# Weighing node rows by counted edges: the counts become the stationary operand behind the first piece

## The reference, cut to what matters

```python
def _L0_gnn_ref(mems, r, W, y, edge_index):
    ...
    deg = jax.ops.segment_sum(w, col, num_segments=MEM_LEN) + SELF_LOOP_W
    dinv = jax.lax.rsqrt(deg)
    norm = dinv[row] * w * dinv[col]
    xw = mems2 @ W
    msg = norm[:, None] * xw[row]
    out = jax.ops.segment_sum(msg, col, num_segments=MEM_LEN)
    out = out + (SELF_LOOP_W * dinv * dinv)[:, None] * xw
    return out
...
x = x + _L0_gnn_ref(_layernorm(x, axis=-1), ...)
x = x + _L0_ffn_ref(_layernorm(x, axis=-1)[None], ...)[0]
```

## Time and profile before

| | us |
|---|---|
| median of three runs | 2783.07 |
| lowest, highest | 2780.23, 2785.92 |
| the profiled execution: its span, first to last instruction | 3123.0 |
| PE, PEld, DVE, ACT, POOL busy in it | 2109.3, 1813.6, 1410.3, 561.5, 1730.5 |

### The profile page before, as it was taken

One profiled execution on the slowest core, in us unless ns is written; L12 is line 12 of the kernel. 1 busy time (PEld: TensorE's weight loads), 2 busy tenths in 40 slices (PEclk: granted clock), 3 DMA queues, 4 the chain that ended last, 5 costly groups with the idle time before them and its releaser, 6 DMA issues. The chain is left out here.

```text
span 3123.0 us, 39685 instructions
## 1 busy us (share of the span) xinstructions
PE 2109.3 (68%) x12106; PEld 1813.6 (58%) x12107; DVE 1410.3 (45%) x3867; ACT 561.5 (18%) x1062; POOL 1730.5 (55%) x1774
## 2 busy tenths in 40 slices
PE   2002665775677657756768868887488689799964
PEld 1002444774466546745757767777477578688754
DVE  5897766225531552254152134444543344344422
ACT  0046100110011001101101112222112223233211
POOL 5731366666666666666666656666034534544354
PEclk7555888988889889888988888998799899899987
DMA  9114222553245325524544556665302212211221
GB/s 238 47 55 142 66 87 88 162 173 93 88 135 177 118 88 162 179 87 128 176 124 151 178 154 188 193 185 177 112 26 61 67 31 66 64 38 64 62 37 23
DMA packets 231940, 350.57 MB, mean 112 GB/s; under 512 B 38888, under 2 KB 165128, under 8 KB 231620
## 3 DMA queue, kind: packets, MB, share of 16 engines
q0 software_dynamic: 79808, 198.30, 22.0%
q1 hardware_dynamic: 151796, 149.91, 15.5%
q10 hardware_dynamic: 144, 0.20, 0.0%
HBM read 296.73 MB, written 56.40 MB: 113 GB/s over the span
## 5 line engine op out<-in xcount | busy, mean ns | idle before, releaser
L633 POOL DMA_INDIRECT arena<-z_table,arena x1248 | 1221.5, 979 | 768.6 <-issue 337.3
L1598 PE MATMUL bank<-arena 128*128 128x128 f32 x4992 | 782.5, 316 | 90.2 <-issue 74.0
L1598 PEld LDWEIGHTS bank<-arena 128*128 128x128 f32 x4992 | 736.7, 228 | 149.8 <-issue 126.8
L1166 DVE TENSOR_TENSOR nodes<-nodes,bank 128x256 f32 x312 | 131.7, 422 | 1076.5 <-remote 749.6
L1609 PE MATMUL bank<-arena 128*128 128x490 bf16 x496 | 169.7, 429 | 313.1 <-DVE arena L1177 287.0
L1823 PE MATMUL bank<-arena 128*128 128x256 f32 (+1 forms) x1472 | 334.1, 385 | 27.1 <-ACT arena L837 24.9
L1811 PE MATMUL bank<-arena 128*128 128x256 f32 (+1 forms) x1472 | 334.9, 388 | 25.2 <-issue 18.6
L1621 PE MATMUL bank<-arena 128*128 128x128 f32 (+1 forms) x1960 | 289.9, 290 | 74.9 <-issue 65.4
L694 POOL DMA_INDIRECT out<-arena x128 | 129.8, 1014 | 355.5 <-DVE arena L1483 343.5
L1811 PEld LDWEIGHTS bank<-arena 128*128 128x128 f32 x1472 | 285.8, 198 | 68.2 <-issue 28.2
L1823 PEld LDWEIGHTS bank<-arena 128*128 128x128 f32 (+1 forms) x1472 | 276.3, 190 | 71.6 <-ACT arena L837 26.9
(11 more groups left out here) (299 smaller groups left out, 1767.5 us busy)
## 6 DMA issues: line engine op xcount, KB each, us to landing
arena<-z_table SPq DMA_DIRECT2D x120, 512.0 KB
arena<-z_table,arena POOLq DMA_INDIRECT x1248
arena<-in_L_ffn_w SPq DMA_DIRECT2D x16, 1024.0 KB
z_table<-nodes SPq DMA_DIRECT2D x14, 896.0 KB, 6.7
x_rows<-nodes SPq DMA_DIRECT2D x98, 128.0 KB
arena<-in_x SPq DMA_DIRECT2D x48, 256.0 KB
out<-nodes SPq DMA_DIRECT2D x96, 128.0 KB
nodes<-in_x SPq DMA_DIRECT2D x12, 896.0 KB, 8.3
```

The costliest lines, as they stand in the source:

```text
L633: nc.gpsimd.indirect_dma_start(gath[:, slot, t, :], None, z_table, bass.IndirectOffsetOnAxis(ap=src_idx[:, tile_at:tile_at + 1], axis=0)). ...
L1166: nc.vector.tensor_tensor(where, where, agg_bank[step % AB][:, 0:D].rearrange("p (k c) -> p k c", k=KD), ALU.add).then_inc(S["agg_added"], 1)
L1598: last = nc.tensor.matmul(agg_bank[i][:, k * P:(k + 1) * P], gath[:, i, t, k * P:(k + 1) * P], sel[:, i, t, :], start=(t == 0), stop=(t == ...
```

## The change

For pieces 1 to 4 the operands change places. For each window PE loads the 128x128 counts as the stationary operand and moves the 256 columns of the z rows past it: one f32 matmul of 256 columns where there were two of 128. The sum in `piece_bank[:, 0:256]` then has the destinations on the partitions. When the piece is closed, ACT copies it to `piece_rows` (`take_piece`), PE transposes both halves into `piece_bank[:, 256:512]` (`turn_piece`), and DVE adds from there. Piece 0 stays as it was. `piece_rows` lies over `count_f`. Two new semaphores (`piece_out`, `piece_turned`) order this. `x_chunk` and `table_out` of a chunk of windows become one, `chunk_moved`, with the sums of both as the numbers waited for.

```diff
         at[0] = count_at
         near_row = carve([8 * P])[0:1, :]
+        at[0] = count_at
+        piece_rows = carve([KD, P])
...
-        x_chunk = [sem(f"x_chunk{c}") for c in range(NZC)]
-        table_out = [sem(f"table_out{c}") for c in range(NZC)]
+        chunk_moved = [sem(f"chunk_moved{c}") for c in range(NZC)]
+        LOADED = [16 * (KD + (c == NZC - 1)) for c in range(NZC)]
+        STORED = [n + 16 * KD for n in LOADED]
...
+            def take_piece(p):
+                act.wait_ge(S["piece_ps"], p + 1)
+                nc.scalar.activation(piece_rows[:, :, :].rearrange("p k c -> p (k c)"), piece_bank[:, 0:D], ACT.Copy).then_inc(S["piece_out"], 1)
+
             for step in range(NG):
                 for n in chunks_of(step):
                     chunk_counts(n)
+                for p in pieces_of(step):
+                    if p:
+                        take_piece(p)
...
             def add_piece(p, step):
...
                 dve.wait_ge(S["agg_added"], adds_through(step))
-                dve.wait_ge(S["piece_ps"], p + 1)
+                if p == 0:
+                    dve.wait_ge(S["piece_ps"], 1)
+                    total = piece_bank[:, 0:KD * (P + 1)].rearrange("p (k c) -> p k c", k=KD)
+                else:
+                    dve.wait_ge(S["piece_turned"], p)
+                    total = piece_bank[:, D:2 * D].rearrange("p (k c) -> p k c", k=KD)
                 where = agg[:, :, bass.ds(base, P)]
-                total = piece_bank[:, 0:KD * (P + 1)].rearrange("p (k c) -> p k c", k=KD)
...
                 for i in range(m):
+                    if p:
+                        last = nc.tensor.matmul(piece_bank[:, 0:D], count_f[:, j, i, 0:P], z_ring[:, j, i, :], start=False, stop=False)
+                        continue
                     for k in range(KD):
...
+            def turn_piece(p):
+
+                pe.wait_ge(S["piece_out"], p)
+                for k in range(KD):
+                    last = nc.tensor.transpose(piece_bank[:, D + k * P:D + (k + 1) * P], piece_rows[:, k, :], ident[:, :])
+                last.then_inc(S["piece_turned"], 1)
+
             for p in range(NP):
+                span = KD * (P + 1) if p == 0 else D
+                whole = piece_bank[:, 0:span]
...
-                nc.tensor.matmul(whole, zeros[:, 0:P], zeros[:, 0:KD * (P + 1)], start=False, stop=True).then_inc(S["piece_ps"], 1)
+                nc.tensor.matmul(whole, zeros[:, 0:P], zeros[:, 0:span], start=False, stop=True).then_inc(S["piece_ps"], 1)
+                if p:
+                    turn_piece(p)
```

More of the change, by code:

```diff
@@ L273, in build @@
         z_ring = carve([2, HB, D])
+        count_at = at[0]
         count_f = carve([2, HB, P + 1])
-        at[0] -= 2 * HB * (P + 1)
+        at[0] = count_at
         near_row = carve([8 * P])[0:1, :]
+        at[0] = count_at
+        piece_rows = carve([KD, P])
         at[0] = counts_at + P * NW // 2
@@ L431, in build @@
                      first_in0 first_in1 first_used starts_ok starts_ps hist_start less_ok bn1_ok shift_ok
-                     mem_ok mem_patched diff_ok dist_ok deg_ok z_ok z_act tick near_ok near_ps chosen_ok zstat_ok zT_ps
+                     piece_out piece_turned mem_ok mem_patched diff_ok dist_ok deg_ok z_ok z_act tick near_ok near_ps chosen_ok zstat_ok zT_ps
                      agg_init sel_ok agg_ps agg_added strip_ok strip_ps strip_added counts_clear count_ok chunk_ps piece_ps
@@ L477, in load_nodes @@
                 for k in range(KD):
-                    sp.dma_start(nodes[:, k, a:b, :], x_win[:, k, a:b, :]).then_inc(x_chunk[c], 16)
+                    sp.dma_start(nodes[:, k, a:b, :], x_win[:, k, a:b, :]).then_inc(chunk_moved[c], 16)
             sp.wait_ge(S["edges_float"], 1)
@@ L487, in _ @@
             sp.wait_ge(S["edges_cleared"], 3)
-            sp.dma_start(nodes[0:LAST, :, NW - 1, :], x_last).then_inc(x_chunk[NZC - 1], 16)
+            sp.dma_start(nodes[0:LAST, :, NW - 1, :], x_last).then_inc(chunk_moved[NZC - 1], 16)
             for c in range(NZC):
@@ L497, in _ @@
                     sp.dma_start(z_win[:, k, c * ZC:(c + 1) * ZC, :],
-                                 nodes[:, k, c * ZC:(c + 1) * ZC, :]).then_inc(table_out[c], 16)
+                                 nodes[:, k, c * ZC:(c + 1) * ZC, :]).then_inc(chunk_moved[c], 16)
             def load_weights(e, j, small=False):
@@ L623, in _ @@
             for c in range(NZC):
-                pool.wait_ge(table_out[c], 16 * KD)
+                pool.wait_ge(chunk_moved[c], STORED[c])
             pool.wait_ge(S["dist_ok"], 2 * NZC)
@@ L998, in _ @@
             for c in range(NZC):
-                dve.wait_ge(x_chunk[c], 16 * (KD + (c == NZC - 1)))
+                dve.wait_ge(chunk_moved[c], LOADED[c])
                 for w in range(c * ZC, (c + 1) * ZC):
@@ L1109, in _ @@
             for c in range(NZC):
-                dve.wait_ge(table_out[c], 16 * KD)
+                dve.wait_ge(chunk_moved[c], STORED[c])
                 with dve.Fori(0, 2) as h:
@@ L1623, in weigh_chunk @@
                 last.then_inc(S["chunk_ps"], 1)
-            whole = piece_bank[:, 0:KD * (P + 1)]
+            def turn_piece(p):
[3 more added lines that the diff above has]
+                last.then_inc(S["piece_turned"], 1)
             for p in range(NP):
+                span = KD * (P + 1) if p == 0 else D
+                whole = piece_bank[:, 0:span]
                 s0, c0, n0 = strip_step[p], chunk_step[p], STRIP0[p]
@@ L1650, in _ @@
                     pe.wait_ge(S["chosen_ok"], 1)
-                nc.tensor.matmul(whole, zeros[:, 0:P], zeros[:, 0:KD * (P + 1)], start=True, stop=False)
+                nc.tensor.matmul(whole, zeros[:, 0:P], zeros[:, 0:span], start=True, stop=False)
                 with pe.Fori(0, (PCH - 1) // BODY - 1) as q:
```

## The result

The changed kernel takes 2787.99 us (median of 20 runs, 2784.69 to 2792.91) against 2784.07 us before (20 runs, 2780.07 to 2788.09). The ratio is 1.0014, with a 95% interval of 1.0008 to 1.0020: slower by 3.9 us, less than the 0.2% that the prediction counted as no change, but outside what this many runs leave open. The forecast was 2781.

The account below looks back on a forecast made before the run. POOL's gathers were taken to bound the kernel at 5.12 us a step. The sum was 2783 - 0 + 0, less a small part of PE's 6 us: 2781, own range 2777 to 2788, overall range 2755 to 2794.

Parts of the forecast that it names:

- POOL's gathers set the steps: In the middle, four gathers of 1.28 us give each of 312 steps a floor of 5.12 us.
- the excess of 0.8 us: Profiled step time above 5.12 us, from late PE signals; taken as a recording cost, some 250 us over 312 steps.
- Rival B: PE's pauses are partly real and shrink with its instructions: 2764, or 2711 with all pauses real; chance 0.28.
- The swap: Chunk matmuls of pieces 1 to 4, 16 pairs a step becoming 8: value 0, at most 72 us gained.
- 0.06 us a step: PE's own gain in a chunk step from the wider matmuls, 6 us in all, beside a POOL that doesn't wait.
- The closings: Four piece ends with copy, transposes and hand-overs: 1.5 us each but covered, so cost 0; upper bound 32 us.
- the hand-overs: Two more signals between engines at each closing, taken at 0.3 us each, bounds nothing and 6.4 us.
- Rival C: Slower: the closing chain reaches POOL in the first steps behind a piece, 6 to 32 us, likeliest 2791; chance 0.16.
- The merged semaphores: `chunk_moved` is waited for at sums reached by the same DMAs as before: 0.
- PE's 6 us: PE's total gain from the wider chunk matmuls, of which a small part was taken off the plain run's time.
- the three chances: Faster 0.28, same 0.56, slower 0.16.
- no change within 0.2%: The forecast case: no measurable change, 2781, within 5.6 us; chance 0.56.

Follow-up runs that it names:

- e12: The changed kernel with pieces 1 to 4 weighing only the last window of each chunk, the other windows' sums left out; 2799.3 us in a single execution.
- e4: The changed kernel with the operand order of before, the closing turn kept; ratio 1.0003 to the kernel before, 2784.18 us.
- e2: The kernel before with only the semaphores merged as in the change; ratio 0.9993, 2780.16 us.
- e3: The changed kernel without `take_piece` and `turn_piece`, sums added with axes exchanged; ratio 1.0033 to the kernel before, 2792.65 us.
- e7: The kernel before with 224 instructions that only signal a semaphore, early in PE's program; ratio 1.0017 to the kernel before.
- e1: The kernel before run and recorded once more, with no edit; ratio 0.9997, 2782.86 us.
- e6: The kernel before with 240 instructions that only signal a semaphore, early in PE's program; ratio 1.0014 to the kernel before.

## Why the prediction was right or wrong

**POOL's gathers set the steps, the excess of 0.8 us was the recording's: right.** The second recording of before, without the late signals, has the chunk step at 4.99 us, a little under the 5.12 that the mean of the earlier trace rows gave. Taking for pauses of the recorder was the choice on which the forecast rested. Rival B is refuted by the unmoved middle and by e12.

**The swap is worth 0: right.** PE's busy time in a chunk stage is equal within 0.4 us; not even the 0.06 us a step is there. PE did not limit the stage either way.

**The closings are worth 0: right, with the hand-overs priced too high.** Piece 4 after, where nothing is cleared, in the timeline:

```profile
1552.60 0.59 PE L1687 MATMUL bank<-zeros 128*128 128x256 f32 x2
1553.23 0.38 ACT L762 ACTIVATE arena<-bank 128x256 f32<-128x256 f32 x1 [5.63 <-PE bank L1687]
...
1553.67 0.44 PE L1647 MATMUL bank<-ident,arena 128*128 128x128 f32 x2 [0.47 <-ACT arena L762]
1554.31 0.42 DVE L1216 TENSOR_TENSOR nodes<-nodes,bank 128x256 f32 x1 [2.91 <-PE bank L1647]
...
1558.29 6.02 PE L1613 MATMUL bank<-arena 128*128 128x128 f32 x32 [4.19 <-DMA gateb_sb<-in_L_ffn_gate_b]
```

and before, second recording:

```profile
1547.88 0.60 PE L1661 MATMUL bank<-zeros 128*128 128x258 f32 x2
...
1548.69 0.42 DVE L1201 TENSOR_TENSOR nodes<-nodes,bank 128x256 f32 x1 [2.09 <-PE bank L1661]
...
1552.90 5.33 PE L1598 MATMUL bank<-arena 128*128 128x128 f32 x32 [4.42 <-DMA gateb_sb<-in_L_ffn_gate_b]
```

From the close's start to `add_piece` are 1.71 us after and 0.81 before: 0.9 us for the turn, where the prediction put 1.5. The copy took 0.38 us where it put 0.47, the transposes 0.44 where it put 0.41, and the hand-overs to ACT and to PE 0.04 and 0.06 where it put 0.3 each. PE's next group waits for the weights in both, 4.2 and 4.4 us of idle time as the last releaser, though it starts 0.7 us later from the close's start in this pair of recordings (5.69 against 5.02). Behind piece 1:

```profile
897.67 5.29 DVE L1203 MEMSET arena<- 128x6272 f32 x1 [1.25 <-issue]
898.25 0.38 ACT L762 ACTIVATE arena<-bank 128x256 f32<-128x256 f32 x1 [5.78 <-PE bank L1687]
898.69 0.44 PE L1647 MATMUL bank<-ident,arena 128*128 128x128 f32 x2 [0.47 <-ACT arena L762]
...
903.79 0.42 DVE L1216 TENSOR_TENSOR nodes<-nodes,bank 128x256 f32 x1 [0.84 <-DVE arena L1203]
```

The sum is turned at 899.13, the clearing ends at 902.96, and `add_piece` comes behind the clearing, as forecast. Rival C got the sign right and the cause wrong: nothing of the closings reaches POOL, and e4, with all four of them, is at 1.0003.

**The merged semaphores are worth 0: right** (e2).

**The step that failed: the sum has no term for the stages behind the groups.** It took the change to end where its last edited line runs ("2783 - 0 + 0, less a small part of PE's 6 us: 2781"), so the feed-forward layer, untouched in the diff, was left at its old time. The runs show a term of +4 to +7 us there: 3.9 by the medians, 6.9 by the stretch behind the last gather in this pair of recordings (890.9 and 897.8). Of the 6.9, 4.6 are in the three jump waits; between the means of the two groups of places the waits differ by 6.0. Of the 7 us from 2781 to 2788 this term is 3.9; 2 us are the small part of PE's 6 us, which did not come, and 1 us is the median before, 2784.07 over 20 runs in place of 2783.07 over three. The direction was missed with it, 2781 for 2788, and of the three chances the largest, no change within 0.2%, is the one that covers the size. The instruction counts that the prediction did work out (784 fewer each for PE and PEld) were used as a check of the profile, not as a displacement of all code behind them.

**Open.** Why -16 and -32 are bad and 0 to +192 are not: a boundary of blocks near the loop's head, so that the head and what follows lie in two blocks, fits the two packets and the length at -32, but no run located the boundary. The third of the three jumps doesn't follow the second: in e3 and e7 it took 5.2 and 5.8 us, as in a good place. The last 1.1 us of the 7.1 are not accounted for. That the queue of the packets is PE's is inferred from their coming in PE's waits, and from their number over the execution, 71 in e1, 69 after with 528 instructions fewer, 68 in e3 with 544 fewer and 72 in e6 with 240 more (e7, with 224 more, has 71). That the jumps wait for code is a reading of these rows; what the runs show is that the place makes the difference. A run with a single closing turned wasn't made, since all four show nothing.

## What to carry to other kernels

When a change shortens or lengthens the instruction stream of an engine, count how far it moves the loops behind it, and read in the profile what their jumps back cost: "issue" idle time at the first instruction of a turn, beside packets of the instruction queue. A difference of one or two thousandths may be only that, and is told from a real one by moving the code without changing the work (some signals in a place where the engine has time). And a stage in which an engine off the bottleneck has slack is not improved by fewer instructions on it: ask for the spacing of the engine that sets the step, here one gather each 1.26 us.

## What the runs showed of the hardware that was not expected

A jump back of a long loop on PE costs 4.8 to 5.9 us of idle time in its good places and 5.2 to 10.5 in the bad ones, each time round; here it has three, 16 us of 2784 at best. One recording of before ran 345 us longer than another of the same kernel (3123.0 and 2778.0), with signals of PE 3 to 6 us late. Besides the gap between its span and the runs' median, two things mark it: "remote" as what ended waits, 749.6 us of them on DVE's line L1166, which no other page of these runs has, and a granted clock of 0.848 where the second recording has 0.904. Halving the weight loads and matmuls of the sum changed PE's busy time by nothing: f32 matmul instructions of 128 columns take 0.12 us each and of 256 columns 0.24, so here the columns alone count (92.49 and 92.85 us busy in 121). In e12, with PE busy 76.61 us of 124 in the chunk stage in place of 92.85 of 121, the granted clock was 0.83 in place of 0.99, and no step got shorter.
